# Two graph layers on one core: the first batch's score transposes, roundings, splits and centring put in another order on four engines

## The reference

```python
h = jnp.maximum(_layernorm(x), 0.0)
Xw = h @ Wv + bv
sj, si = Xw @ aw[:d, 0], Xw @ aw[d:, 0]
e = leaky_relu(sj[:, None, :] + si[:, :, None] + ab[0], 0.2)
alpha = A * jnp.exp(e)
T = alpha / (jnp.sum(alpha, axis=-1, keepdims=True) + 1e-12)
H, Xk = 0, h
for k in range(3):
    H = H + Xk @ Wk[k] + bk[k]
    Xk = T @ Xk                       # per batch
x = x + relu(H)
h = jnp.maximum(_layernorm(x), 0.0)
Ah = A + I;  dh = rsqrt(sum(Ah, -1))
x = x + relu(dh * Ah * dh @ h @ kernel + bias)
```

## Time and profile before

| | before |
|---|---|
| median of 3 runs | 760.78 us (758.87 to 761.71) |
| the profiled execution | 760.17 us, span 758.4 us |
| PE busy | 746.5 us (98%) |
| DVE, ACT, POOL busy | 624.3 (82%), 535.7 (71%), 185.8 us (24%) |
| mean granted TensorE clock | 0.997 of full speed |

### The profile page before, as it was taken

The page is one execution under the profiler, slowest core; times in us unless marked ns, Lnnn a source line. Parts: engine busy times, 40 slices in busy tenths (PEclk is TensorE's granted clock), DMA queues, the critical chain, the costliest instruction groups (busy, mean ns, idle before and its releaser), DMA issues.

```text
span 758.4 us, 14017 instructions
## 1 busy us (share of the span) xinstructions
PE 746.5 (98%) x5091; PEld 686.8 (91%) x5091; DVE 624.3 (82%) x1415; ACT 535.7 (71%) x1044; POOL 185.8 (24%) x192
## 2 busy tenths in 40 slices
PE   8899999999999999999999999999999999999997
PEld 8688988989899898999989999899988999889986
DVE  6898788878888789887989778897888878986665
ACT  3898795668955789567885679767696667955451
POOL 3022240322403133130322214122150322402230
PEclk9999999999999999999999999999999999999999
DMA  6666448644587265762568625766348754556521
GB/s 213 218 249 225 144 157 295 202 174 154 175 284 244 91 183 194 262 225 90 187 211 281 222 93 168 252 234 223 112 153 289 211 194 132 172 171 194 157 67 56
DMA packets 63909, 143.32 MB, mean 189 GB/s; under 512 B 6768, under 2 KB 32864, under 8 KB 63840
## 3 DMA queue, kind: packets, MB, share of 16 engines
q1 hardware_dynamic: 55072, 111.75, 44.9%
q10 hardware_dynamic: 8768, 30.68, 12.0%
HBM read 133.96 MB, written 8.45 MB: 188 GB/s over the span
## 4 chain that ended last, share of the span: by engine, by line
PE 88%; DVE 6%; DMA 2%; ACT 2%; issue 1%; POOL 1%; SPq 0%; DVEq 0%; ACTq 0%
PE acc L1189 14%; PE acc L1191 14%; PE acc L1190 14%; PE da L1054 13%; PE db L1054 7%; PE tp L1155 4%; PE tp L1157 4%; PE tp L1156 4%; PE da L1155 4%; PE da L1157 4%; PE da L1156 4%; DVE t_raw L816 1%; DVE t_lo L821 1%; DMA tg_a<-adj_t_dram 1%; DMA h<-x_dram 1%
## 5 line engine op out<-in xcount | busy, mean ns | idle before, releaser
L1189 PE MATMUL acc<-g_hi,t_hi 128*128 128x256 f32 (+1 forms) x976 | 276.7, 283 | 0.1
L1191 PE MATMUL acc<-g_hi,t_lo 128*128 128x256 f32 (+1 forms) x976 | 275.2, 282 | 0.0
L1190 PE MATMUL acc<-g_lo,t_hi 128*128 128x256 f32 x976 | 274.6, 281 | 0.0
L1189 PEld LDWEIGHTS acc<-g_hi,t_hi 128*128 128x128 f32 x976 | 183.7, 188 | 1.1 <-DVE g_lo L790 0.3
L1190 PEld LDWEIGHTS acc<-g_lo,t_hi 128*128 128x128 f32 x976 | 184.3, 189 | 0.3
L1191 PEld LDWEIGHTS acc<-g_hi,t_lo 128*128 128x128 f32 x976 | 184.1, 189 | 0.0
L404 POOL TENSOR_TENSOR g_lo<-tmp,g_hi 128x256 fp32r<-128x256 f32 x64 | 59.7, 933 | 264.5 <-ACT g_hi L588 264.5
L827 DVE TENSOR_TENSOR a_lo<-a_raw,a_hi 128x512 fp32r<-128x512 f32 x128 | 93.9, 748 | 23.8 <-ACT a_hi L576 23.6
L533 ACT ACTIVATE tg_e<-si,sij 128x256 f32<-128x256 f32 x256 | 109.1, 498 | 0.3 <-DMA si<-si_rows_dram 0.3
L576 ACT CAST a_hi<-a_raw 128x512 fp32r<-128x512 f32 x128 | 76.6, 616 | 26.0 <-DVE a_raw L867 17.9
L410 POOL TENSOR_TENSOR hs_lo<-tmp,hs_hi 128x256 fp32r<-128x256 f32 x64 | 59.8, 955 | 89.8 <-ACT hs_hi L473 89.8
(11 more groups left out here) (169 smaller groups left out, 1607.6 us busy)
## 6 DMA issues: line engine op xcount, KB each, us to landing
a_raw<-adj_dram SPq DMA_DIRECT2D x64, 512.0 KB, 4.4
a_raw<-adj_z_dram SPq DMA_DIRECT2D x64, 512.0 KB, 4.1
tg_a<-adj_t_dram ACTq DMA_DIRECT2D x58, 512.0 KB, 4.2
x_o<-x_dram SPq DMA_DIRECT2D x64, 128.0 KB, 3.4
out_dram<-x_o SPq DMA_DIRECT2D x64, 128.0 KB, 3.9
x_nat<-x_dram SPq DMA_DIRECT2D x28, 256.0 KB, 4.7
xt<-x_t_dram SPq DMA_DIRECT2D x28, 256.0 KB, 5.1
si<-mean_rows_dram SPq DMA_DIRECT2D x7, 512.0 KB, 4.8
```

Source lines behind the costliest of these rows:

```text
L1189: nc.tensor.matmul(acc[:, s, 0:n], l_hi, r_hi, start=(jt == 0), stop=False)
L1190: nc.tensor.matmul(acc[:, s, 0:D], l_hi, r_lo, start=False, stop=False)
L1191: ins = nc.tensor.matmul(acc[:, s, 0:n], l_lo, r_hi, start=False, stop=(jt == NT - 1))
```

## The change

Nothing is computed otherwise. In the first batch: the third warm-up shrinks from 14 to 5 transposes; two small adds that make `cst` go ahead of the split of `wb`; `first_transposes(3)` and then `first_si(0)` stand ahead of the third pair of products; `wl_hi` is rounded, and the second half of `si` copied, inside the dense loop; four of the eight `first_p0` move into it; units of T are pulled forward in the DVE list; `t_high` of unit u - 1 stands ahead of `exponent` of unit u; the centring of batch 1 begins one chunk sooner, and row tiles 3 and 4 one chunk later.

```diff
-    FIRST_LEAKY_D, FIRST_EXP_D, FIRST_HIGH_D = {0: 1, 4: 2, 6: 3}, {1: 1, 5: 2, 7: 3}, {2: 0, 3: 1}
-    FIRST_PROD_D, FIRST_LOW_D = {2: 1, 6: 2}, {4: 0, 5: 1}
-    FIRST_HIGH_U, FIRST_PROD_U, FIRST_LOW_U = {0: 6, 1: 7}, {0: 5, 1: 6, 2: 7}, {0: 4, 1: 5, 2: 6, 3: 7}
+    FIRST_LEAKY_D, FIRST_EXP_D, FIRST_HIGH_D = {2: 2, 6: 3}, {0: 1, 5: 2, 7: 3}, {1: 0, 3: 1}
+    FIRST_PROD_D, FIRST_LOW_D = {1: 1, 6: 2}, {2: 0, 4: 1}
+    FIRST_HIGH_U, FIRST_PROD_U, FIRST_LOW_U = {1: 7}, {0: 6, 1: 7}, {0: 5, 1: 6, 2: 7}
-    FIRST_ROWS_U, FIRST_ROWS_D = {2: (0,), 3: (1,), 4: (2,), 5: (3,), 6: (4,)}, {0: (5,), 1: (6,), 3: (7,)}
+    FIRST_ROWS_U, FIRST_ROWS_D = {2: (0,), 3: (1,), 4: (2,), 6: (3,), 7: (4,)}, {0: (5,), 1: (6,), 3: (7,)}
-    WARM = (24, 4, 14)
+    WARM = (24, 4, 5)
# ACT, batch()
-                    if i >= NT - 2 and not last:
-                        centred_hi(i - (NT - 2), b + 1)
+                    rounding = {NT - 3: 0, NT - 1: 1} if b == 0 else {NT - 2: 0, NT - 1: 1}
+                    if i in rounding and not last:
+                        centred_hi(rounding[i], b + 1)
                     if i == 0:
                         leaky(b, NU - 1)
+                        if b == 0:
+                            t_high(0, NU - 2, False)
                         exponent(b, NU - 1)
# ACT, start
-            nc.scalar.copy(wl_hi[:, :, :], wk_raw[:, 3]).then_inc(weights_rounded, 1)
             first_si_copy(0)
             leaky(0, 0)
-            first_si_copy(1)
             exponent(0, 0)
+            leaky(0, 1)
             for t in range(NT):
                 dense0(0, t)
+                if t == 2:
+                    nc.scalar.copy(wl_hi[:, :, :], wk_raw[:, 3]).then_inc(weights_rounded, 1)
+                if t == 4:
+                    first_si_copy(1)
...
+                t_high(0, u - 1, False)
                 exponent(0, u)
-                t_high(0, u - 1, False)
# DVE, batch()
-                    if i == NT - 1 and not last:
+                    if i == (NT - 2 if b == 0 else NT - 1) and not last:
                         centred_lo(0, b + 1)
-                    if i in (NT - 3, NT - 2) and not last:
-                        centre(i - (NT - 3), b + 1)
+                    centring = {NT - 4: 0, NT - 2: 1} if b == 0 else {NT - 3: 0, NT - 2: 1}
+                    if i in centring and not last:
+                        centre(centring[i], b + 1)
+                    if i in low and b == 0:
+                        t_low(b, low[i])
                     if i in prod:
                         t_prod(b, prod[i])
-                    if i in low:
+                    if i in low and b > 0:
                         t_low(b, low[i])
# DVE, start
+            then(nc.vector.tensor_tensor(cst[:, 2:3], v_s[:, KD, 0:1], v_s[:, KD, 1:2], ALU.add))
+            then(nc.vector.tensor_tensor(cst[:, 0:1], cst[:, 2:3], ab_s, ALU.add))
             dve.wait_ge(weights_rounded, 1)
...
             first_lo(0)
             dve.wait_ge(rstd_first, 2)
             norm0(2)
-            then(nc.vector.tensor_tensor(cst[:, 2:3], v_s[:, KD, 0:1], v_s[:, KD, 1:2], ALU.add))
-            then(nc.vector.tensor_tensor(cst[:, 0:1], cst[:, 2:3], ab_s, ALU.add))
             first_lo(1)
...
-            for t in FIRST_P0[3:]:
-                first_p0(t)
+            first_p0(FIRST_P0[3])
             t_prod(0, 0)
             for t in range(NT):
                 dve.wait_ge(g2_hi_done, t + 1)
                 nc.vector.tensor_copy(p1[:, t, :], da[:, t % 2, 0:D])
                 g2_low(0, t)
+                if t < HJ:
+                    first_p0(FIRST_P0[HJ + t])
...
-            for u in (3, 4):
-                t_prod(0, u)
-                t_low(0, u - 1)
+            t_prod(0, 3)
+            t_low(0, 2)
+            t_low(0, 3)
+            t_prod(0, 4)
             stats0_of(1, NT - 2)
             stats0_of(1, NT - 1)
             moments0(1)
+            t_low(0, 4)
+            t_prod(0, 5)
# PE, start
             first_transposes(3)
+            first_si(0)
             first_pair(2)
-            first_si(0)
             first_pair(3)
```

## The result

| | before | changed |
|---|---|---|
| median of 20 runs each, same chip | 760.26 us (758.87 to 761.71) | 761.43 us (760.64 to 762.57) |
| the profiled execution | 760.17 us, span 758.4 | 761.23 us, span 759.4 |
| ratio of the runs | | 1.0018, 95% interval 1.0011 to 1.0025 |

What follows compares the result with a forecast made beforehand. TensorE (PE), busy 98% of the span, was taken as the bound; -0.7 -0.1 -1.9 +0.9 +2.4 = +0.6 on 760.17 gave 760.8 profiled, 761.0 forecast for the median; range 758.0 to 763.2, the forecast's own 760.2 to 761.8.

Steps and rivals of the forecast that it cites:

- Step 1: Start of the kernel: first products near 12.2, slowed by the 0.50 clock until 13.0; 0.7 us gained.
- Steps 2 and 3: First batch: score transposes at 16.4, 2.2 us sooner; dense tiles keep the gain at 0.8, PE ending them at 34.3.
- Step 4: First hop: 1.9 us more gained, 2.7 in all, PE free at 58.3.
- Step 5: Batch 1's centring: PE idles 2.1 for the split input, starts the first tile at 60.4; 1.8 us of gain left.
- Step 6: Behind batch 1's first tile: 2.4 us given back, with a 1.5 wait for `db` and the chunk load 1.6 later.
- The sum: Whole kernel: the terms give +0.6 us, which neither grows nor shrinks later, as PE hardly idles from there on.
- The kept gain: Batch 1's first tiles: roundings and chunk load come in time, the 1.8 us gain stays; 758.4 to 760.2; chance 0.25.
- The late load of unit 5: First hop: this load's queue is 1.8 us slower; +1.0 to +2.5, 761.8 to 763.3; chance 0.15.
- The low clock: Start: the clock stays at the 1.2 GHz level, slower by over 0.5%, 3.8 us; chance 0.04.

Runs made afterwards that it cites:

- e12: Kernel before with only the back part (batch 1's centring, rounding and split sooner, row tiles 3 and 4 later); ratio 1.0020.
- e7: Kernel before with only the third warm-up cut from 14 to 5 transposes; ratio 1.0003.
- e11: Changed kernel with the third warm-up back at 14 transposes; ratio 1.0017.
- e5: e2 with 20 useless transposes filling PE's stand ahead of batch 1; ratio 1.0016.
- e2: Changed kernel with only batch 1's first split on DVE moved back behind chunk 6; ratio 1.0013.
- e3: Changed kernel with all of batch 1's first centring, rounding and splitting back at the old places, row tiles as changed; ratio 1.0026.
- e4: e2 with row tile 0 taken into the dense loop at tile 4, row tiles 1 to 3 behind chunks 2 to 4; ratio 1.0015.
- e8: Changed kernel with the edits of e1 and e3 together, leaving only the front of the change; ratio 1.0022.
- e1: Changed kernel with row tiles 3 and 4 of the first batch back behind chunks 5 and 6; ratio 1.0008.
- e6: Changed kernel with row tile 0 in the dense loop, row tiles 1, 2, 3 behind chunks 2, 3, 5, so ACT rounds right after centring; ratio 0.9988.
- e9: Changed kernel with row tile 0 in the dense loop, 1 ahead of the last unit's rounding, 2 to 4 behind chunks 2, 3, 5; 758.35 us, ratio 0.9978.
- e10: e4 with 20 transposes filling PE's stand ahead of batch 1; ratio 0.9999.

## Why the prediction was right, and where it was not

The predicted 761.0 and its own range of 760.2 to 761.8 hold the profiled 761.23 and the median 761.43; the forecast's mechanism, a gain of 2.7 us by the end of the hop that is given back in batch 1's first tiles, is what the trace shows. Two of its terms were wrong and cancelled.

- *Step 1, start: the mechanism was not there.* It took the 0.50 of the earlier trace rows as a property of the start. It belonged to that execution: e12 has the same start and e7 the same but for the warm-up, both had 1.00 from 9.6 to 13.0, and both reached the first dense tile at 21.6 to 21.7, like before with its 21.52. So the low clock of that execution had cost the start nothing, the changed kernel had no slow products, and the warm-up's length (e7, e11) is no term at all. The start is 1.3 sooner all the same, 20.21 for the predicted 20.7: from first product to first dense tile the changed kernel needs 8.2, e7 10.2, of which 1.37 is the stand for the second `g_lo`. The two `cst` adds ahead of it took 0.69 and 0.65 in e7; at their new place they took 0.15 and 0.16 (the prediction had 0.2 each), and that stand is gone. No run moved the adds alone. The rule of the Trainium skill on transposes (TensorE: Matmul & The Clock Gate, Part 4, PE-mode transpose), against which the prediction took the trace's side, disagrees with e5 too.
- *Steps 2 and 3* came at 15.91 (16.4), 20.27 for `t_prod(0)` (20.7), waits of 0.47, 1.02 and 0.39 us at tiles 4, 5 and 7 (0.7, 1.0, 0.6). But the dense loop did not keep the start's gain: from first dense tile to first matmul of the hop it took 14.06 (20.21 to 34.27) where it took 13.67 (21.52 to 35.19), 0.4 lost where 0.1 was to be gained.
- *Step 4*: the hop's end 2.9 sooner (2.7). The hop itself gained 1.96 (1.9), a hit; the sum up to here was right by luck, since the start brought 0.5 more and the dense loop 0.5 less than forecast.
- *Step 5*: 60.26 behind 1.78 (60.4 behind 2.1). DVE stood 0.80, not 1.1. Right, and worth more than the prediction saw: without this earlier split the stand is 2.8 to 3.3 and the clock falls (e2, e3, e4, e8). Undoing it does not bring back the 2.4 of step 6.
- *Step 6*: `db` at 65.36 behind 1.35 (1.5), the load at 64.36 (64.4), second hop 0.65 later (0.6). From batch 1's first tile to the second hop that is 2.6 given back (2.4): PE's step ahead of 65.36 is 1.5 longer than a step without a wait, and a wait of 0.42 at 70.28, gone in e1, makes another 0.6 longer. Mis-sized: the wait of the diagonal for its chunk, 0.83 where up to 0.5 was given; the load landed 4.2 us after its issue.
- *The sum* had +0.6 where profiles differ by 1.06 and runs by 0.8 to 1.9. The last 0.4 come behind the second hop, where "neither grows nor shrinks" stood. From there to the last matmul before took 675.17 and the changed kernel 675.58, but e7, whose program from there on is that of before, took 676.49, and e6 675.06. One profile each can't tell this part from the scatter of executions; whether the change adds anything there stays open.
- *Rivals.* The kept gain (0.25) failed on the row tiles, as its "against" said: e6 and e9 show that it was to be had by moving them where ACT stands idle. The late load of unit 5 (0.15) did not come in the changed kernel's profile; in e9, where the load went out as in the changed kernel, it landed 0.50 late. The low clock (0.04) did not come at the start. It did come in four of the variants, at a place that the prediction did not look at, PE's stand ahead of batch 1, and cost 1.2 to 1.6 us (e10 against e4), less than the 3.8 of this rival.

## What to carry to other kernels

A stage that ends sooner ahead of a fixed wait only lengthens the stand; price the stand too, since a long one can bring the clock down, which cost 1.2 to 1.6 us here (e10 against e4). When a chain of handshakes crosses two strict lists, look first for filler (here the row sums) between its links and move that into idle time earlier in the list, not the links. And compare profiles from a common event, not from zero, and ask whether a low clock in one profile is in the others before building a term on it.

## What was not expected of the hardware

- Stands of PE at full clock: after 1.78 and 1.79 us (changed, e1) the granted clock stayed at 1.00; after 2.80, 2.83, 3.13 and 3.33 (e4, e2, e8, e3) it went to 0.50, at 61.0 to 63.7 in their spans, in e3, e4 and e8 only after PE had begun again (0.3 to 1.2 us after), and came back between 3 and 3.5 us later. It never fell in the 1.35 at `db`. But in the profile of before it fell at 9.6, behind a stand of only 0.48 us:

```profile
8.93 1.76 PE L1046 MATMUL tp<-ident,h 128*128 128x128 f32 x8 [0.48 <-DVE h L741]
```

  In e12, with the same list up to there, PE did not stand at this place and the clock did not fall. So the length of one stand does not by itself tell whether the level falls. Filled with transposes (e5, e10) the stand ahead of batch 1 left it at 1.00. The Trainium skill (TensorE: Matmul & The Clock Gate, Part 4, PE-mode transpose) says that transposes do not count as busy in the same way; these two runs disagree. In the profile of before PE ran nothing but transposes from 7.8 to 13.0: the fall at 9.6 would fit the page, the rise at 13.0 would not.
- The split of 512 columns on DVE took 1.22 instead of 0.69 us when POOL's subtraction had begun 0.16 sooner (e2; 1.22, 1.22 and 1.23 in e4, e5 and e10, and 1.21 in e3, where POOL had begun 0.27 sooner). The Trainium skill (SBUF — State Buffer, Who interferes with whom) says that a DVE operation with two SBUF inputs and a GpSimd one that reads SBUF exclude each other, and that the later one waits for the whole of the other; the trace agrees: a free subtraction of POOL takes 0.74, so in e2 it would be over at 60.72, the split's own 0.69 from there would end at 61.41, and it ended at 61.36.
